# Perceiver, second layer: normalization and query projection inside the narrow attention's opening, two sets of key buffers

## The reference

```python
xn = layernorm(x)                       # mean and variance of each row, eps 1e-5
q, k, v = xn @ Wq, ctx @ Wk, ctx @ Wv   # 16 heads of 16
p = softmax(mask(q @ k.T / 4))
x = x + (p @ v) @ Wo
```

## Time and profile before

| | us |
|---|---|
| median of 3 runs | 3967.9 (3961.36 to 3968.45) |
| profiled execution, own time | 3966.35 |
| profiled execution, span of the core | 3964.5 |
| PE busy | 3556.0 (90%) |
| DVE busy | 2504.1 (63%) |
| ACT busy | 2288.3 (58%) |
| POOL busy | 1672.5 (42%) |

### The profile page before, as it was taken

The page is one execution under the profiler, slowest core; times in us unless marked ns, Lnnn a source line. Parts: engine busy times, 40 slices in busy tenths (PEclk is TensorE's granted clock), DMA queues, the critical chain, the costliest instruction groups (busy, mean ns, idle before and its releaser), DMA issues. The chain is left out here.

```text
span 3964.5 us, 81166 instructions
## 1 busy us (share of the span) xinstructions
PE 3556.0 (90%) x30262; PEld 2603.4 (66%) x30262; DVE 2504.1 (63%) x3811; ACT 2288.3 (58%) x4298; POOL 1672.5 (42%) x1381
## 2 busy tenths in 40 slices
PE   6899999999999999999787985799999987769689
PEld 4687778778877888887546983455555543334578
DVE  5666666666666666665274113587878877559688
ACT  3666666666666666666352112366666666526455
POOL 1587777777777777777332002111011000015332
PEclk9999999999999999999888997799999999879899
DMA  6677677776777676665113565788878754100111
GB/s 241 256 293 286 252 267 271 273 274 256 277 273 263 256 268 246 245 244 197 42 11 133 217 240 197 195 179 170 169 178 169 155 79 64 20 29 1 31 44 35
DMA packets 231413, 723.01 MB, mean 182 GB/s; under 512 B 47325, under 2 KB 128221, under 8 KB 162141
## 3 DMA queue, kind: packets, MB, share of 16 engines
q1 hardware_dynamic: 228336, 709.44, 56.5%
q0 software_dynamic: 2688, 8.39, 0.6%
HBM read 623.47 MB, written 94.24 MB: 181 GB/s over the span
## 5 line engine op out<-in xcount | busy, mean ns | idle before, releaser
L805 POOL TENSOR_TENSOR wa_acc<-wa_acc,wa_probs 128x512 f32<-128x512 f32 x960 | 1259.0, 1311 | 458.8 <-ACT wa_probs L650 343.6
L715 DVE TENSOR_REDUCE wa_mx<-wa_ps_x 128x1 f32<-128x512 f32 x1024 | 658.6, 685 | 361.1 <-PE wa_ps_x L503 361.0
L650 ACT ACTIVATE wa_probs<-wa_ps_s 128x512 f32<-128x512 f32 x1024 | 530.6, 603 | 551.1 <-PE wa_ps_s L546 550.6
L1444 DVE TENSOR_REDUCE na_mx<-na_ps_m 128x2 f32<-128x1024 f32 x512 | 614.1, 1220 | 202.7 <-PE na_ps_m L1265 199.3
L1389 ACT ACTIVATE na_probs<-na_ps_s 128x512 f32<-128x512 f32 x1024 | 555.9, 595 | 316.3 <-PE na_ps_s L1285 314.0
L642 ACT ACTIVATE wa_ps_s<-wa_m_wide 128x512 f32<-128x512 f32 x1024 | 578.8, 615 | 0.0
L524 PE MATMUL wa_ps_o<-wa_probs,wa_values 128*64 128x256 f32 x4096 | 468.7, 381 | 0.0
L524 PEld LDWEIGHTS wa_ps_o<-wa_probs,wa_values 128*64 128x64 f32 x4096 | 285.5, 137 | 158.5 <-ACT wa_probs L650 23.8
L468 PE MATMUL wa_ps_x<-w_k_ctx,wa_w_k 128*128 128x512 f32 x1488 | 381.0, 403 | 6.0 <-DMA w_k_ctx<-ctx_split 5.7
L491 PE MATMUL wa_ps_x<-wa_w_v,w_v_ctx 128*128 128x256 f32 x2880 | 363.8, 283 | 0.1
L491 PEld LDWEIGHTS wa_ps_x<-wa_w_v,w_v_ctx 128*128 128x128 f32 x2880 | 356.9, 191 | 6.3 <-issue 0.5
(11 more groups left out here) (400 smaller groups left out, 5769.7 us busy)
## 6 DMA issues: line engine op xcount, KB each, us to landing
w_k_ctx<-ctx_split SPq DMA_DIRECT2D x248, 1024.0 KB, 7.0
w_v_ctx<-ctx_split SPq DMA_DIRECT2D x120, 1024.0 KB, 8.1
na_keys<-k_rows SPq DMA_DIRECT2D x384, 128.0 KB
na_ctx<-ctx_split SPq DMA_DIRECT2D x43, 1024.0 KB, 12.0
ctx_split<-w_stage SPq DMA_DIRECT2D x32, 1024.0 KB, 5.0
first_keep<-in_ctxT SPq DMA_DIRECT2D x32, 512.0 KB, 11.2
ge_w_b<-in_w_rows SPq DMA_DIRECT2D x8, 2048.0 KB, 7.8
k_rows<-na_k_high SPq DMA_DIRECT2D x64, 256.0 KB, 2.8
```

The source lines that it names most:

```text
L650: act.activation(probs[:, c % R:c % R + 2, h * SQ:(h + 1) * SQ], ps_s[n % BANKS][:, :].rearrange("p (c n) -> p c n", c=2), ACT.Exp).then_i ...
L715: dve.tensor_reduce(mx[:, half, h, k:k + 1], ps_x[banks[h]][:, :], AX.X, ALU.max).then_inc(m_taken, 1)
L805: pool.tensor_tensor(to[:, :], to[:, :], probs[:, c % R, :], ALU.add).then_inc(summed, 1)
L1444: dve.tensor_reduce(mx[:, half, :, k], ps_m[n % 2][:, :, :], AX.X, ALU.max).then_inc(m_taken, 1)
```

## The change

1. The two query programs before the narrow attention are gone. Their work is done in its opening, with the same arithmetic, except that a unit is scaled and rounded in one ACT instruction, and DVE takes the low part straight from PSUM. DVE normalizes first; PE turns the eight row tiles after the values of block 0, then makes units 0 and 1; units 2 and 3 follow the values of block 1. Rows, weights and stages lie in tiles that the opening does not use yet (`probs`, `keys[2]`, `ov`).
2. Odd blocks of the opening mask and round their keys into a second set of tiles (`other`, in `probs`), with store semaphores of their own, so a block waits for the store two blocks back. In the loop over the pairs the first set alone is used, as before.
3. Around it: the weights' high part moves from DVE to ACT, POOL's memset for the values' ones goes ahead of its part of the split, context 1 is loaded ahead of the edge index, PE's waits for the selectors move behind the opening, the first two pairs' queries are loaded after block 2 (once the units are stored), and the edge marks are made after blocks 1, 2, 4 and 6 and stored after blocks 2, 3, 5 and 7. The loop over a block's query units has a name of its own, `units_at`.

```diff
+        other = [probs[:, 6 + i, :] for i in range(4)]
+        def key_buffers(n, m):
+            if n < FIRST and n % 2:
+                return other[m], other[2 + m].bitcast(F32R)
+            return k_masked[m][:, :], k_high[m][:, :]
+        def stored_before(n, stored):
+            last = n - 2 if n < FIRST else n - 1
+            return stored[last % 2], 1 + 16 * (last // 2 + 1)
+        def units_at(n):
+            return [u for u in (2 * n, 2 * n + 1) if u < UNITS]
...
             load_ctx(0, False)
+            sp.dma_start(wq, w_q.rearrange("(k p) n -> p k n", p=P)).then_inc(wq_in, 16)
...
+            load_ctx(1, False)
             sp.dma_start(edge_index, consts["key_index"].partition_broadcast(4)).then_inc(edge_in, 16)
-            for n in range(1, 4):
+            for n in range(2, 4):
                 load_ctx(n, False)
...
-            sp.wait_ge(q_fixed, 1 + 6)
-            load_queries(0)
-            load_queries(1)
-            store_edges(0)
             for n in range(FIRST):
                 store_keys(n, 0)
                 store_keys(n, 1)
                 if n + 4 < FIRST:
                     load_ctx(n + 4, False)
-                if n in (2, 4, 6):
-                    store_edges(n // 2)
+                for u in units_at(n):
+                    store_queries(u)
+                if n == 2:
+                    store_edges(0)
+                    for i in range(2):
+                        sp.wait_ge(q_out[i], 16 * UNITS)
+                    sp.wait_ge(q_fixed, 1 + 6)
+                    load_queries(0)
+                    load_queries(1)
+                if n in (3, 5, 7):
+                    store_edges((n - 1) // 2)
                 if n == 3 or n == 7:
                     load_keys(0, n // 4)
...
-            pe.wait_ge(sel_in, 1 + 32)
-            pe.wait_ge(fixed, 1 + 1)
-            pe.wait_ge(q_fixed, 1 + 6)
             pe.wait_ge(high_split, 1 + 2)
             pe.wait_ge(low_split, 1 + 2)
             for n in range(FIRST):
...
+                if n == 0:
+                    for t in range(NT):
+                        turn_row(t)
+                for unit in units_at(n):
+                    project_unit(unit)
                 if n >= 5:
+                    if n == 5:
+                        pe.wait_ge(q_low_ready, UNITS)
                     maximum(0, 2 * (n - 5))
...
             turn_maximum(0)
+            pe.wait_ge(sel_in, 1 + 32)
+            pe.wait_ge(fixed, 1 + 1)
...
+            act.activation(warm, ident[:, 0:1], ACT.Sqrt)
+            act.wait_ge(inv_ready, 1)
+            act.activation(rstd, inv, ACT.Sqrt).then_inc(root_ready, 1)
+            act.wait_ge(w_in, 1 + 32)
+            for j in range(2):
+                act.activation(w_high[:, j, :, :], w_land[:, j, :, :], ACT.Copy).then_inc(high_split, 1)
             act.wait_ge(ones_ready, 1 + 1)
             for n in range(FIRST):
                 take_high(n, 0)
                 take_high(n, 1)
...
+                if n == 0:
+                    for t in range(NT):
+                        take_row(t)
+                for unit in units_at(n):
+                    unit_high(unit)
...
             def mask_keys(n, m, bank):
                 b, k = divmod(n, CG)
                 dve.wait_ge(kp_done, 1 + 2 * n + m + 1)
-                dve.wait_ge(hi_ready, 1 + max(2 * (n - 1) + m + 1, 0))
-                dve.wait_ge(lo_stored[m], 1 + 16 * n)
+                if n >= 2:
+                    dve.wait_ge(hi_ready, 1 + 2 * (n - (2 if n < FIRST else 1)) + m + 1)
+                    dve.wait_ge(*stored_before(n, lo_stored[m]))
...
+            normalize()
             dve.memset(ps_o[:, :, :], 0.0).then_inc(fixed, 1)
-            dve.wait_ge(w_in, 1 + 32)
-            for j in range(2):
-                split_weights(j)
...
-            mark_edges(0)
             for n in range(FIRST):
                 mask_keys(n, 0, ps_s[0])
                 mask_keys(n, 1, ps_s[1])
-                if n in (1, 3, 5):
-                    mark_edges(n // 2 + 1)
+                for unit in units_at(n):
+                    unit_low(unit)
+                if n in (1, 2, 4, 6):
+                    mark_edges(n // 2)
...
+            pool.memset(v_all[0][:, :, :, DH:VW], 1.0).then_inc(ones_ready, 1)
             for j in range(2):
                 pool.wait_ge(high_split, 1 + j + 1)
...
-            pool.memset(v_all[0][:, :, :, DH:VW], 1.0).then_inc(ones_ready, 1)
...
-        queries("x1", a["L1_xattn_Wq"], D, 0.25, q_high1, q_low1)
```

More of the change, by code:

```diff
@@ L1031, in narrow_attention @@
         w_land = probs[:, 0:2, :].rearrange("p c (k n) -> p c k n", k=KD)
+        xT = probs[:, 2:6, :].rearrange("p c n -> p (c n)").rearrange("p (k n) -> p k n", k=KD)
+        xn = probs[:, 6:10, :].rearrange("p c n -> p (c n)").rearrange("p (t n) -> p t n", t=NT)
+        wq = probs[:, 10, :].rearrange("p (k n) -> p k n", k=KD)
+        other = [probs[:, 6 + i, :] for i in range(4)]
+        q_stage = [[keys[2][:, (2 * part + i) * 512:(2 * part + i + 1) * 512] for i in range(2)] for part in range(2)]
         q = [s.sb(f"q{i}", [P, SQ], F32R) for i in range(3)]
@@ L1041, in narrow_attention @@
         ov = s.sb("ov", [P, SQ])
+        stats, mv = ov[:, 0:6 * NT].rearrange("p (t n) -> p t n", t=NT), ov[:, 64:64 + 2 * NT].rearrange("p (t n) -> p t n", t=NT)
+        inv, rstd, t1, t2, rfin = (ov[:, 96 + i * NT:96 + (i + 1) * NT] for i in range(5))
+        warm = ov[:, 160:161]
         rden = s.sb("rden", [W, SQ])
@@ L1049, in narrow_attention @@
         edge_index, edge_sb = spare[:, 0:SK], spare[:, SK:2 * SK].bitcast(F32R)
+        z = Scope(nc, stack, "nq")
+        pt = pq = [ps_m[0][:, i, :] for i in range(2)]
+        wq_in = z.sem("wq_in")
+        stats_ready, aggregated, chain, inv_ready, root_ready = (
+            z.sem(n) for n in ("stats_ready", "aggregated", "chain", "inv_ready", "root_ready"))
+        xn_ready, transposed, evacuated = z.sem("xn_ready"), z.sem("transposed"), z.sem("evacuated")
+        q_done, q_high_ready, q_low_ready = z.sem("q_done"), z.sem("q_high_ready"), z.sem("q_low_ready")
+        q_out = [z.sem(f"q_out{i}") for i in range(2)]
         w_in, const_in, edge_in = s.sem("w_in"), s.sem("const_in"), s.sem("edge_in")
@@ L1307, in add_up, with turn_row, project_unit @@
                 pe.matmul(ps_p[0:W, SQ:2 * SQ], sel_den[:, :], ov[:, :], start=True, stop=True).then_inc(summed, 1)
-            pe.wait_ge(sel_in, 1 + 32)
-            pe.wait_ge(fixed, 1 + 1)
-            pe.wait_ge(q_fixed, 1 + 6)
+            def turn_row(t):
+                pe.wait_ge(xn_ready, t + 1)
+                if t >= 2:
+                    pe.wait_ge(evacuated, t - 1)
+                for k in range(KD):
+                    ins = pe.transpose(pt[t % 2][:, k * P:(k + 1) * P], xn[:, t, k * P:(k + 1) * P], ident[:, :])
+                ins.then_inc(transposed, 1)
+            def project_unit(n):
+                if n == 0:
+                    pe.wait_ge(wq_in, 16)
+                    pe.wait_ge(evacuated, NT)
+                if n >= 2:
+                    pe.wait_ge(q_high_ready, n - 1)
+                    pe.wait_ge(q_low_ready, n - 1)
+                for k in range(KD):
+                    ins = pe.matmul(pq[n % 2], wq[:, k, n // 2 * P:(n // 2 + 1) * P], xT[:, k, n % 2 * 512:(n % 2 + 1) * 512],
+                                    start=(k == 0), stop=(k == KD - 1))
+                ins.then_inc(q_done, 1)
             pe.wait_ge(high_split, 1 + 2)
@@ L1403, in _ @@
                     take_values(n, half, first_bank(n, half))
+                if n == 0:
+                    for t in range(NT):
+                        take_row(t)
+                for unit in units_at(n):
+                    unit_high(unit)
             take_maximum(0)
+            for m in range(2):
+                act.wait_ge(hi_stored[m][1], 1 + 16 * (FIRST // 2))
+                act.wait_ge(lo_stored[m][1], 1 + 16 * (FIRST // 2))
             for a in range(G):
```

77 lines of the change are left out of this document (61 added, 16 removed).

## The result

The changed kernel takes **3939.93 us** (median of 4 runs, 3935.99 to 3945.86) against 3967.21 for the kernel before (4 runs): **ratio 0.9935, 95% interval 0.9922 to 0.9949**, so faster by 27 us, 0.65%. Forecast were 3939 us, and faster with 0.94. Five more runs, taken beside the last experiments, gave 3940.83, ratio 0.9938 (0.9924 to 0.9952).

The account below looks back on a forecast made before the run. Mostly one engine working at a time before a slow opening, then PE stalls behind DVE's late masks, were taken as the bound; -36.4 + 11.5 - 12.4 + 8.6 - 0.3 = -29.0 us gave 3939 us, range 3930 to 3951.

Parts of the forecast that it names:

- Start, -36.4: Stage start: PE's first key projection moves from 2431.81 to 2395.4, released by POOL's weight split; -36.4 us.
- Queries in PE, +11.5: Blocks 0 and 1: query work in PE's queue adds 8.1 and 3.4 us, +11.5 us.
- Edge wait: One edge tile: mark 1 waits for store 0, PE idles before block 4, mark 2 costs 1.0; +8.6 us.
- block 3's stores are ready later than that: SP's queue after block 2: twelve query-load issues take 4 to 6 us beside DVE's wait; nothing charged.
- Two key sets: Blocks 0 to 5: a second buffer set removes PE's stalls from late masks; up to -12.4 us, taken whole.
- Rival B: Second buffers don't help: DMA engines are full and the wait only moves; -16.6 us, 3951 us, chance 0.16.
- - 0.3: Masks of blocks 9 and 10: their small waits for stores go; -0.3 us.
- The loop: Loop over the 32 pairs: not edited, forecast to keep its length.
- Rival A: No edge wait: edge store lands in some 2 us, marks cost next to nothing; -37.6 us, 3930 us, chance 0.22.
- C: Normalization: POOL's memsets and DVE hold each other up, 2.7 us on POOL's chain; 3942 us, chance 0.06.
- D: Slower: edge chain at marks 1, 2, 3 becomes the opening's clock; 3978 us at 16 us per landing, chance 0.04.
- E: Comes out even: the same edge chain at 12 to 13 us per landing; chance 0.02.

Follow-up runs that it names:

- queries outside: Changed kernel with the two query programs put back ahead of the narrow attention, all else as changed; 3957.54 us, ratio 0.9982.
- all-orders kernel: Changed kernel, two edge tiles, edge stores and pair 1's keys before context loads, queries after keys, POOL's split before ones, DVE's index wait later; 3935.52 us, ratio 0.9923.
- one key set: Changed kernel with the second set of key buffers taken out; 3945.80 us, ratio 0.9946.
- pair 1's keys first: Changed kernel with pair 1's key loads issued ahead of two 1 MB context loads; 3939.69 us, ratio 0.9928.
- edge store first: Changed kernel with each edge store issued ahead of the 1 MB context load in SP's queue; 3934.57 us, one run.

## Why the prediction was right, and where its steps were not

The time was right, and the sign: 3939.93 and 3940.83 us against 3939. The steps:

**Start, -36.4: right to a tenth.** From the first statistics to PE's first projection 48.79 us became 12.41, and POOL was the releaser. The edge index landed late but inside its bound: the first mask waited 3.00 us for it and began at 2399.2 on the clock of before (2399.6 at worst), and as said ACT's idle time took that up.

**Queries in PE, +11.5: 10.5** (7.5 + 3.0); the two blocks themselves were 0.8 longer, so block 2 began at 2420.1 on the clock of before, forecast 2420.4. Up to here the schedule holds to 0.3 us.

**Edge wait: the mechanism was there, the term was mis-sized.** Mark 1 began at 2434.5 (forecast 2434.4), PE idled 5.71 us (5.5). Mark 2 waited 4.59 us where I had charged 1.0, and mark 3, which I had charged nothing, 6.33, since its store landed in 9.2 us. Yet with all these waits gone the time did not change. "+8.6 us" was really about 0: what PE saves there it spends at the first keys of pair 0, whose loads need block 3's stores, and these stand behind twelve query loads in SP's queue. I had walked past them, charging nothing: "block 3's stores are ready later than that". With the loads moved the maxima end 4.7 us sooner in the mean. That is measured with the edge waits gone; no run moves the loads and keeps the waits, so how the two would share this cost is not shown.

**Two key sets, "up to -12.4 us", taken whole: 4 to 6.** The waits on tiles went, as said. But the 12.4 assumed that PE then runs stall-free to block 5's maxima, and those need loads that need the stores of block 3, their marks and the queries. Rival B, "the wait only moves", had a good part of this term right, though what holds the keys up at first is the order of the queue and not only full engines.

**The sum was right because faults cancel.** The kernel with queries outside parts the start's -36.4: its PE starts 8.1 us sooner than before, so the reordered start is worth 8.1 and the two programs gone are worth 28.4 (40.81 to 12.41). Less the 10.5 that PE pays for the query work, moving it in is worth 17.9; the ratios of the two kernels say 18, the openings 21.2 (189.22 to the mean of 168.0). This part was forecast right. For the rest I had -12.4 + 8.6 - 0.3 = -4.1. From PE's first projection to the opening's end it is 146.4 and 141.8 us in the two profiles of before, 158.2 and 152.3 in the two of the changed kernel: 11.1 more in the mean, and the query work is 11.3 of that (10.5 and the 0.8). So the rest is worth about 0, within some 5 us. The second set brings 4 to 6 instead of 12.4, the edge waits cost nothing instead of 8.6, and the query loads, charged nothing, cost some 4.7. That these nearly cancel is luck; the gain, 25 us by the openings and 27 by the medians, is somewhat less than the 29.0.

**The loop.** It was to keep its length, and its passes are the same to 0.1 us but for chance: the -8.3 of the two first profiles are one pass of 32.4 us, which two other kernels and the repeated kernel before have too and the changed one does not, and the last two passes. Without the scatter of loop and start, 25 us are left from the opening (193.0, the mean of the two befores, to 168.0), and that is what the ratios say.

Rival A's time was wrong as its mechanism was: without an edge wait the kernel is no faster. C: the next section. D and E did not come up; the gain stands far from their point. What stays open: PE's middle wait for keys, 3.2 to 4.9 us in all kernels behind the change, is for loads that the queue issues behind block 7's stores; nothing was tried on it. That PE's sooner start brings nothing in the all-orders kernel was not separated from that kernel's other edit, the edge stores.

## What to carry to other kernels

Before a removed wait is booked, follow the engine to the next thing that it consumes, and ask when that lands and what stands ahead of it in the queue that issues it: here two waits in a row, 28 us and 20 us of idle rows, were worth some 5 and about 0. If two terms of a sum are covered by the same later event, forecast them as one. The issue order of one DMA queue was worth 6.6 us more without touching any arithmetic, and forecasting when a wait ends told more than forecasting how long it is.

## What the runs showed of the chip that I had not expected

**A pass of the loop at the lower clock.** Four profiles have one or two passes of 32.4 us at places that move (in both of before, with one key set, and with pair 1's keys first). The windows view of pair 1's keys first, passes around the first one (columns as above):

```profile
3184.20:3212.90 28.70, 23.94 (x264) 13.41 (x264) 22.00 (x24) 18.97 (x36) 0.61 (x2) 1.00 0.48 66
3212.90:3245.30 32.40, 25.86 (x238) 12.24 (x237) 22.19 (x23) 17.99 (x34) 0.61 (x2) 0.79 0.54 69
3245.30:3273.20 27.90, 20.97 (x240) 10.49 (x242) 22.00 (x23) 17.99 (x34) 0.61 (x2) 1.00 0.38 52
```

Between passes at 1.00, the full 2.4 GHz, one is granted 0.79 on average, so part of it ran at 1.2 GHz; PE's busy time goes from 20.97 to 25.86 us and the pass from 27.7 to 32.4. A cut of 3 us from within the pass shows the lower level itself:

```profile
3238.00:3241.00 3.00, 2.25 (x16) 1.18 (x18) 1.56 (x3) 1.69 (x4) 0.00 (x0) 0.50 1.31 147
```

The pass ahead, 28.70 us, is as long as in the other kernels. What brought the clock down is not shown. It is 4.7 us that no kernel owns, more than most single terms above.

**DVE and POOL side by side.** The eight normalizing writes took 2.68 us alone and 3.37 beside POOL's fills, and the fills 2.21 and 2.29 us instead of 2.09 and 2.10. So rival C's price, all 2.7 us on POOL, did not come: POOL lost 0.3. In the all-orders kernel POOL's split stands ahead of the fills, and the eight writes took 5.03. Rows of the changed kernel's POOL first, then of the all-orders kernel, where one write has a row of its own:

```profile
2390.24 2.21 POOL L1655 MEMSET na_q<- 4x256 f32 x6 [7.92 <-issue]
2392.50 2.29 POOL L1650 MEMSET na_q<- 2x256 f32 x6
...
2393.19 1.26 POOL L1660 TENSOR_TENSOR na_w_low<-na_probs,na_w_high 128x512 fp32r<-128x512 f32 x1
2393.29 2.25 DVE L1549 TENSOR_SCALAR na_probs<-g_x,na_ov 128x256 f32<-128x256 f32 x1
2394.39 1.00 POOL L1662 MEMSET na_v_all<- 128x512 f32 x1
```

The first write, beside the second half of the split and the fill of ones, took 2.25 us; most of the others took 0.48, as in the changed kernel, and 0.41 alone. So the two can hold each other up, and nearly all of the 5.03 over the 3.37 is that one write. Whether the 0.07 us of the others comes from POOL is not shown, since they also write into another tile. The Trainium skill, "SBUF — State Buffer", section "Who interferes with whom", has the later of the two blocked for the whole instruction when VectorE's takes the port pair that it shares with GpSimd; the one long write agrees in kind, the others beside the fills lose far less than a fill's length (0.3 us).

**A store of four partitions under load.** 64 KB landed 4.2 to 13.9 us after issue, in the changed kernel and with the edge store first; the key stores of the earlier trace rows, 256 KB each, have 2.0 as their least. The DMA engines' busy share over these six landings was 0.88 to 1.09, and 0.93 in the longest, so it does not tell the long ones from the short ones; what does is not shown.
